# One more Mamba state by transposition: state 13 leaves VectorE for ScalarE and TensorE, with three places in the hand-written order moved

## The reference

```python
# d = 256 inner channels, n = 16 states, one step per token
dA = jnp.exp(d_t[:, :, None] * A)                       # decay of each state
h  = h * dA + (d_t * u_t)[:, :, None] * b_t[:, None, :] # the scan
y  = jnp.einsum('bdn,bn->bd', h, c_t)                   # sum over the 16 states
...
y = (y + xc * Dp) * jax.nn.silu(z)
return y @ out_w.T
```

## Time and profile before

| | |
|---|---|
| median of three runs | 2614.42 us (2611.18 to 2614.97) |
| profiled execution, its own time | 2614.2 us |
| its span | 2612.1 us |
| mean granted TensorE clock | 0.962 |
| POOL busy over the span | 2198.4 us (84%) |
| DVE busy | 2240.6 us (86%) |
| PE busy | 2227.8 us (85%) |
| ACT busy | 1895.3 us (73%) |

### The profile page before, as it was taken

The page is one execution under the profiler, slowest core; times in us unless marked ns, Lnnn a source line. Parts: engine busy times, 40 slices in busy tenths (PEclk is TensorE's granted clock), DMA queues, the critical chain, the costliest instruction groups (busy, mean ns, idle before and its releaser), DMA issues.

```text
span 2612.1 us, 48904 instructions
## 1 busy us (share of the span) xinstructions
PE 2227.8 (85%) x15840; PEld 1908.7 (73%) x15840; DVE 2240.6 (86%) x3430; ACT 1895.3 (73%) x3628; POOL 2198.4 (84%) x1402
## 2 busy tenths in 40 slices
PE   4899999668888898888888888888988768999992
PEld 3799999446776777776776766766766647999992
DVE  8766666789999999999999999999999887666666
ACT  4355555389999989999999999999999543555551
POOL 3677777379999999999999999999999936777772
PEclk8999999889999999999999999999999978999996
DMA  7011112533333333333333333333333240111126
GB/s 249 21 48 49 49 50 50 144 94 105 110 103 104 107 106 102 107 107 101 111 101 103 112 100 105 111 107 104 106 107 107 85 161 24 50 49 49 49 49 211
DMA packets 156821, 248.73 MB, mean 95 GB/s; under 512 B 22082, under 2 KB 66018, under 8 KB 155874
## 3 DMA queue, kind: packets, MB, share of 16 engines
q1 hardware_dynamic: 137568, 202.79, 26.1%
q0 software_dynamic: 18208, 37.26, 5.3%
q10 hardware_dynamic: 866, 6.43, 0.6%
HBM read 213.10 MB, written 33.29 MB: 94 GB/s over the span
## 4 chain that ended last, share of the span: by engine, by line
PE 37%; POOL 19%; DVE 15%; issue 14%; ACT 10%; DMA 4%; ACTq 0%; DVEq 0%; POOLq 0%; SPq 0%
PE bank L1351 10%; POOL buf L548 8%; DVE buf L917 7%; PE bank L1547 6%; PE bank L1372 6%; PE bank L1422 4%; POOL token_outputs L497 4%; POOL buf L487 4%; PE bank L1522 3%; PE bank L1332 3%; ACT over L1164 3%; DMA buf<-state_rows 2%; ACT scaled L1197 2%; DVE buf L904 2%; POOL buf L535 2%
## 5 line engine op out<-in xcount | busy, mean ns | idle before, releaser
L548 POOL TENSOR_TENSOR buf<-buf 128x1024 f32<-128x1024 f32 x512 | 1199.9, 2374 | 32.4 <-PE bank L1547 27.0
L917 DVE TENSOR_TENSOR_SCAN buf<-over,bank 128x512 f32<-128x512 f32 x832 | 953.8, 1200 | 4.9 <-PE bank L1522 2.7
L1164 ACT ACTIVATE over<-wgu,negA 128x510 f32<-128x510 f32 x832 | 541.5, 709 | 40.3 <-DVE buf L917 28.8
L1547 PE MATMUL bank<-id_sb,buf 128*128 128x128 f32 x4096 | 515.8, 279 | 6.8 <-POOL buf L548 6.8
L1547 PEld LDWEIGHTS bank<-id_sb,buf 128*128 128x128 f32 x4096 | 478.2, 144 | 57.2 <-issue 46.6
L1351 PE MATMUL bank<-parts 128*128 128x256 f32 x3408 | 447.6, 288 | 17.3 <-DVE buf L767 9.2
L1351 PEld LDWEIGHTS bank<-parts 128*128 128x128 f32 x3408 | 420.7, 193 | 36.7 <-issue 36.7
L1197 ACT ACTIVATE scaled<-wd_sb,I 128x256 f32<-128x256 f32 x896 | 377.3, 497 | 22.6 <-PE bank L1522 22.5
L497 POOL DMA_INDIRECT token_outputs<-buf,slot_out x284 | 299.5, 1055 | 87.9 <-issue 84.0
L487 POOL DMA_INDIRECT buf<-token_rows,slot_token x284 | 284.5, 1002 | 95.4 <-issue 82.5
L1522 PE MATMUL bank<-id_sb,scaled 128*128 128x128 f32 x1792 | 256.0, 280 | 88.3 <-ACT scaled L1197 38.2
(11 more groups left out here) (170 smaller groups left out, 3061.6 us busy)
## 6 DMA issues: line engine op xcount, KB each, us to landing
buf<-state_rows SPq DMA_DIRECT2D x608, 256.0 KB, 3.2
token_rows<-buf SPq DMA_DIRECT2D x32, 256.0 KB, 2.3
wd_sb<-token_outputs SPq DMA_DIRECT2D x16, 512.0 KB, 4.0
buf<-token_outputs SPq DMA_DIRECT2D x16, 512.0 KB, 4.8
buf<-token_rows,slot_token POOLq DMA_INDIRECT x284, 2.5
token_outputs<-buf,slot_out POOLq DMA_INDIRECT x284
out<-X SPq DMA_DIRECT2D x16, 256.0 KB, 3.6
wgu<-wgT ACTq DMA_DIRECT2D x1, 2048.0 KB, 9.1
```

The lines of the kernel that those rows point to most:

```text
L548: pool.tensor_tensor(hC[:, b, :].rearrange("p (c w) -> p c w", c=C), hs[:, b, :].rearrange("p (c w) -> p c w", c=C), Cs[:, b, :].unsqueeze ...
L917: V.tensor_tensor_scan(hs[:, b, w], dA[:, b, c, :, :].rearrange("p s t -> p (s t)"), source, 0.0, ALU.mult, ALU.add).then_inc(s[f"scan_don ...
L1164: ins = A.activation(dA[:, n % R, c, :, 1:], delta[r][:, c * W:(c + 1) * W].rearrange("p (s t) -> p s t", s=S)[:, :, 1:], ACT.Exp, scale=n ...
L1547: ins = M.matmul(bank[4 + q // 2][:, at:at + P], hC[:, n % R, c * W + q * P:c * W + (q + 1) * P], id_sb[:, :], is_transpose=True, start=Fa ...
```

## The change

State 13 becomes a turned state: its `product` (L889) and its `spread` (L1489) go, four scalings on ScalarE and eight transposes on TensorE come. Since banks 2 and 3 would be in use by state 12, its transposes go to banks 0 and 1 (`TURNED_LOW`), after the scan of state 11. State 13 is scaled at step 10, and the scaling of state 14 moves from 12 to 11, which is ahead of the copies of the gated rows. The sum of state 14 moves from step 18 to step 17 (step 1 of the next unit); that of state 15 stays at 18.

```diff
-SUM_AT = {6: (0, 1, 2), 7: (3, 4), 9: (5, 6), 11: (7, 8), 12: (9,), 13: (10,), 15: (11,), 16: (12, 13), 18: (14,
-    15)}
+SUM_AT = {6: (0, 1, 2), 7: (3, 4), 9: (5, 6), 11: (7, 8), 12: (9,), 13: (10,), 15: (11,), 16: (12, 13), 17: (14,),
+    18: (15,)}
...
-TURNED_UNITS = (2, 4, 6, 8, 10, 12, 14)
-SCALE_AT = {0.5: (0, 4), 1.5: (0, 6), 3.0: (0, 8), 6.0: (0, 10), 9.0: (0, 12), 12.0: (0, 14), 15.5: (1, 2)}
+TURNED_UNITS = (2, 4, 6, 8, 10, 12, 13, 14)
+TURNED_LOW = (13,)
+SCALE_AT = {0.5: (0, 4), 1.5: (0, 6), 3.0: (0, 8), 6.0: (0, 10), 9.0: (0, 12), 10.0: (0, 13), 11.0: (0, 14), 15.5: (1, 2)}
...
+            if n in TURNED_LOW:
+                return bank[c]
...
+                low = n in TURNED_LOW
+                last = max((m for m in TURNED_UNITS if m < n and m not in TURNED_LOW), default=TURNED_UNITS[-1] - NS)
+                if not low:
+                    wait(pe, s["scan_done1"], u * NS + last + 1)
                 for c in range(C):
+                    if low:
+                        wait(pe, s[f"scan_done{c}"], u * NS + n - 1)
+                    else:
+                        wait(pe, s["mul_done"], 2 * (vector_before(u, n) - 1 + c))
```

More of the change, by code:

```diff
@@ L1516, in turn_back @@
                 pe.wait_ge(s["scaled_done"], turned_before(u, n) + 1)
-                last = max((m for m in TURNED_UNITS if m < n), default=TURNED_UNITS[-1] - NS)
-                wait(pe, s["scan_done1"], u * NS + last + 1)
+                low = n in TURNED_LOW
+                last = max((m for m in TURNED_UNITS if m < n and m not in TURNED_LOW), default=TURNED_UNITS[-1] - NS)
+                if not low:
+                    wait(pe, s["scan_done1"], u * NS + last + 1)
                 for c in range(C):
-                    wait(pe, s["mul_done"], 2 * (vector_before(u, n) - 1 + c))
+                    if low:
+                        wait(pe, s[f"scan_done{c}"], u * NS + n - 1)
+                    else:
+                        wait(pe, s["mul_done"], 2 * (vector_before(u, n) - 1 + c))
                     for q in range(G):
```

## The result

The change makes the kernel slower: 2678.4 us as the median of four runs (2677.34 to 2681.33) against 2614.06 of the kernel before beside it (2611.18 to 2614.97), a ratio of 1.0252 (95% interval 1.0238 to 1.0267). Forecast: 2671, range 2622 to 2695. The span of the profiled execution grows from 2612.1 to 2675.6, by 63.5 us.

What follows compares the result with a forecast made beforehand. POOL, 98.2% busy, and a second loop through PE's full run were taken to bound the kernel. Late copies cost 3.8 us a pair, 15 pairs 57 us on 2614.2, other terms 0: 2671 us, range 2622 to 2695.

Steps and rivals of the forecast that it cites:

- The second loop: Beside POOL: copies, 18 us of PE without slack, gate, scans, step size, scaling of 12, decays, copies; 96.37 us a pair.
- The copies late by two scalings: Scalings of 13 and 14 ahead of ScalarE's copies start PE's run 2.5 us later in direction 0, 1.9 in direction 1.
- The pair: Two units, one per direction, get longer by 2.5 + 1.9 - 0.6 = 3.8 us, from 96.4 to 100.2.
- The 0.6 us of slack behind the gate: In direction 1 DVE waits 0.60 us after the gate for POOL's product of state 3; this absorbs delay once a pair.
- The bound from below: Only one 1.60 us scaling counts per direction, after slack of 0.76 and 0.90 and the 0.60: 0.9 us a pair.
- The sum of the delays: Copies exist from unit 1, PE's preparation up to unit 30: 15 pairs x 3.8 = 57 us in all.
- the unknown that stood beside the sum without a term: PE's clock may fall when PE waits; a 3.5 us stretch at half pace costs up to 1.7 us.
- The fourth rival: The delay is worse as clock falls enter the loop, 27 us more: 2698 us and above; chance 0.06.
- VectorE's relief: Two products removed at state 13, 38 to 44 us over 32 units, spent waiting for PE: worth 0, at most 32.4.
- TensorE's exchange: One spread goes, eight transposes come at step 12, +0.56 us a unit, while PE waits for copies: worth 0, else 18.
- The sum of state 14: Its 0.87 us on PE moves ahead of a convolution; the gate stays: worth 0, at most 28 us either way.
- What the profile was to show: PE waits about 2 us for ScalarE's copies in some 30 units; gates 100 us a pair; POOL waits nearly 5.

Runs made afterwards that it cites:

- run 2: The changed kernel with ScalarE's copies of the gated rows at step 11 instead of 12, ahead of state 14's scaling: 2614.86 us, 1.0004.
- run 1: The changed kernel with state 14's scaling back at step 12, behind the copies of the gated rows; state 13 stays turned: 2626.76 us, 1.0046.
- run 4: The kernel before with only state 14's scaling moved from step 12 to 11, ahead of the copies of the gated rows: 2629.14 us, 1.0057.
- run 7: The kernel before with the sum of state 0 at step 4 instead of 6 on PE: 2606.10 us, 0.9973.
- run 6: The kernel of run 2 with, in addition, the sum of state 0 at step 4 instead of 6: 2610.07 us, 0.9994.
- run 3: The kernel before with only the sum of state 14 moved from step 18 to 17: 2614.20 us, 1.0002.
- run 8: The changed kernel with copies at 10, output product and `du` transposes at 11.6, sums 7, 8 and 0 earlier: 2622.86 us, 1.0040.
- run 10: The kernel before with copies and `du` at 10, output product at 11.6, `du` transposes at 12.6, sums 7, 8, 0 earlier: 2648.26 us, 1.0135.

## Why the prediction was right, point by point

- **The second loop.** The step that the rest hung on, that PE's run from `turn_du` to the gate has no slack and that late copies move its start, holds. Run 2 moves the copies alone and gets the 64 us back; runs 1 and 4 put one scaling ahead of them, with and without state 13, and lose 14 and 16 us. One thing is to be read with care: "its start waits for the copies" is true only of late copies. In before the last wait ahead of the run is 0.42 us of the `spread` of state 13 for DVE's scan, and the copies are done 0.76 us before; in run 7 the run starts by the scaling of 12. The copies take over once they are later than their slack.
- **The copies late by two scalings.** Predicted start 3.67 + 3.20 = 6.87 us behind the scaling of 12, measured 6.88. PE's run in direction 0 starts 1587.17 - 1579.09 = 8.08 us behind it, against 1542.96 - 1537.47 = 5.49: +2.6, predicted +2.5. In direction 1 without a fall of the clock it starts 30.74 us behind the gate, against 29.35: +1.4, predicted 1.9 - 0.6 = 1.3.
- **The pair.** Predicted 100.2, measured 51.11 + 48.93 = 100.04 in undisturbed pairs. The 0.6 us of slack behind the gate is gone, as taken; run 7 measures it from the other side, 96.37 - 95.77 = 0.60.
- **The bound from below.** One scaling after all slack was to cost 0.9 a pair, 14 us; runs 1 and 4 measure 13.6 and 15.9. The agreement is partly luck: their undisturbed pairs are 0.47 and 0.48 longer, 7 us in 15 pairs, and most of the rest is the clock, which the bound left out.
- **The sum of the delays, mis-sized.** "15 x 3.8 = 57 us", measured 64.3. The undisturbed pairs give 15 x 3.67 = 55 of it. The rest is the unknown that stood beside the sum without a term, the falls of TensorE's clock. In after 10 of the 30 distances between gates are 0.9 to 1.7 us longer than their like, about 15 us together, and each of the ten holds a fall; in before two are, by 1.6 and 1.7. That is about 12 more. Some 4 us are given back between the last two gates and behind them, which leaves 63.5 on the span. The prediction said that more waiting may bring falls, or that they may come where PE waits anyway, and put no number to it; both happened (last section). The fourth rival was this, with twice the size.
- **VectorE's relief, worth 0.** Right by runs 2 and 6. By the rule of the Trainium skill (Perfetto Trace Analysis, section Optimizing Scalar/DVE Operations) offloading a saturated VectorE may make sense; here VectorE was 97.2% busy and lost 39 us of work, and the time moved by +1.65 us (2614.86 against 2613.21) where the order was mended. The trace doesn't bear the rule out for this case.
- **TensorE's exchange, worth 0.** Right: run 2 has it in full and is at the time of before.
- **The sum of state 14, worth 0.** Right by run 3.
- **What the profile was to show.** PE waits for ScalarE in 30 units, as said, about 2.4 us in direction 0 and 1.8 in direction 1 where no fall comes before it; "about 2 us in each" was right. POOL's waits 4.5 a pair ("nearly 5"), DVE's work -39 ("some 41"), ACT's +47 ("some 51"). DVE's waits at scan 14 were foreseen and not sized: 113.8 us, almost three times its saved work, since the delay of PE's run shows up there as well.

Left open: what a fall of the clock costs by itself. No run held the clock up with the order unchanged, so its share of the 64 us is read from the distances between gates and from where the falls lie, and not from an experiment.

## What to carry to other kernels

In a list issued in order, work added to an engine with spare time is paid by whatever stands behind it there. So before placing it, look for the item behind it that another engine waits for, and its slack: here 0.8 us, against 3.2 us put ahead. An engine at 98% is not yet the only bound; look for an unbroken run of another engine between two waits that repeats once a unit (here 18 us of PE), and follow both ends of it. And a mended order must be followed to the next wait behind: runs 8 and 10 took one wait away and met another, `du` on GpSimd and a spread on PE. A wait that a change puts on TensorE can have a second price: five times its clock fell right behind it here, at 1.6 us each.

## What the runs showed of the hardware

TensorE's clock falls about as often before and after, and the falls cost differently. Read in pieces of 4 us from 590 to 2045, the granted clock dips below 0.9 in 12 stretches before and 15 after. Before, two of 30 gate distances are longer by over 1 us, and each holds two falls; after, ten are by 0.9 or more, and each holds one or two. Of the 19 others up to the 30th gate only two hold a fall.

Five of the ten are of a kind that before doesn't have. Their fall comes right behind PE's wait of 2.4 us for the copies, inside its full run (at 677, 879, 1384, 1790 and 1991), and each makes the distance 1.6 us longer (52.7 against 51.1). One of them (columns as in the earlier trace rows):

```profile
1790.00:1794.00 4.00, 4.00 (x24) 4.00 (x23) 0.00 (x0) 1.55 (x3) 4.00 (x3) 0.57 0.58 138
```

So part of the 12 us hangs on the late copies too, since the wait ahead of these falls is theirs. The two falls that cost nothing, at 1073 and 1681, lie ahead of that wait in direction 0, and the wait takes them up: it is 0.80 and 0.81 us there instead of 2.43.

One of the other five, with PE in order of time, then the stretch:

```profile
1629.75 1.84 PE L1530 MATMUL bank<-id_sb,scaled 128*128 128x128 f32 x8 [1.86 <-ACT scaled L1200]
1631.38 2.88 PE L1555 MATMUL bank<-id_sb,buf 128*128 128x128 f32 x16
```

```profile
1629.00:1633.00 4.00, 3.25 (x16) 3.25 (x17) 4.00 (x5) 4.00 (x9) 4.00 (x3) 0.62 0.52 184
```

The engine had waited 1.86 us and then ran at the lower level (1.2 instead of 2.4 GHz): eight transposes took 1.84 us and not 1.04, sixteen 2.88 and not 1.91, together 1.8 us more. The distance to the next gate (1605.36 to 1655.87), which holds a second fall near 1620, is 50.5 where its like is 48.9.

The same fall has another price in another order. In before, four distances of direction 0 hold one fall some 15 us behind the gate, and they are 0.1 to 0.2 us longer than their like (48.84 to 48.91 against 48.76). In run 4, where only the scaling of 14 has moved, seven hold such a fall, and they are 0.9 to 1.0 longer (50.41 to 50.52 against 49.52). A pair of gates of before with the stretch between them, then one of run 4, where the clock from 853 to 857 is 0.57:

```profile
1415.80 1.29 DVE L877 TENSOR_TENSOR buf<-bank,wgu 128x512 f32<-128x512 f32 x2 [0.60 <-PE bank L1547]
...
1464.71 1.29 DVE L877 TENSOR_TENSOR buf<-bank,wgu 128x512 f32<-128x512 f32 x2 [0.60 <-PE bank L1547]
```

```profile
1430.00:1434.00 4.00, 3.49 (x20) 3.25 (x21) 4.00 (x5) 4.00 (x10) 4.00 (x3) 0.70 0.27 70
```

```profile
838.19 1.29 DVE L877 TENSOR_TENSOR buf<-bank,wgu 128x512 f32<-128x512 f32 x2 [0.60 <-PE bank L1547]
...
888.70 1.29 DVE L877 TENSOR_TENSOR buf<-bank,wgu 128x512 f32<-128x512 f32 x2 [0.60 <-PE bank L1547]
```

That before has slack in the second loop at this place and run 4 has none is the reading that fits; it is argued from these distances and not tested by itself.
